# Five changes of order in a two-block transformer kernel: keys of the first group emptied earlier, a transpose between two halves of an up projection, two layer norms on POOL, one V projection in halves, the sigmoid moved up

## What is computed

```
block 0:  h = film(rmsnorm(x, norm1_w), cond, film1_w, film1_b)
          Q, K, V = h @ q_w + q_b, h @ k_w + k_b, h @ v_w + v_b       # one head of 128
          x = x + softmax(Q K^T * 128**-0.5) V @ proj_w + proj_b
          h = film(rmsnorm(x, norm2_w), cond, film2_w, film2_b)
          x = x + gelu(h @ mlp_w1 + mlp_b1) @ mlp_w2 + mlp_b2
block 1:  mod = silu(cond) @ ada_w.T + ada_b                          # six vectors per sequence
          h = layernorm(x) * (1 + scale_msa) + shift_msa
          x = x + gate_msa * (attention(h, 16 heads of 8, masked) @ proj_w.T + proj_b)
          h = layernorm(x) * (1 + scale_mlp) + shift_mlp
          x = x + gate_mlp * (gelu_tanh(h @ fc1_w.T + fc1_b) @ fc2_w.T + fc2_b)
```

## Time and profile before

| | us |
|---|---|
| median of 3 runs | 193.1 |
| lowest, highest | 192.03, 194.94 |
| the profiled execution | 191.69 |
| its span, first to last instruction | 189.9 |
| busy in the span: PE | 173.1 |
| PE weight loads | 134.2 |
| DVE | 121.1 |
| ACT | 107.7 |
| POOL | 98.7 |

### The profile page before, as it was taken

How to read it: one execution, slowest core, us unless ns; L and a number is a source line. 1 busy time by engine, 2 the same in 40 slices (tenths; PEclk the granted TensorE clock), 3 DMA queues, 4 the chain that set the end, 5 groups by cost and what they waited for, 6 DMA issues and landing times.

```text
span 189.9 us, 5687 instructions
## 1 busy us (share of the span) xinstructions
PE 173.1 (91%) x2250; PEld 134.2 (71%) x2250; DVE 121.1 (64%) x357; ACT 107.7 (57%) x272; POOL 98.7 (52%) x166
## 2 busy tenths in 40 slices
PE   6876989999699999889999999996997999999993
PEld 6744877587276698677678777875886765678592
DVE  0693598978005069768756876699489665596233
ACT  2336957862683751577577756673774785723500
POOL 5599949899900805994004333675145086691000
PEclk9999999999999999999999999998899999999999
DMA  5999999412650300300110000100000000001103
GB/s 126 345 430 423 433 412 431 177 43 52 217 224 0 114 0 3 116 5 5 57 60 3 7 35 31 57 5 2 5 7 7 2 3 0 5 0 55 59 0 110
DMA packets 5190, 19.31 MB, mean 102 GB/s; under 512 B 556, under 2 KB 1148, under 8 KB 3836
## 3 DMA queue, kind: packets, MB, share of 16 engines
q1 hardware_dynamic: 4844, 18.27, 25.0%
q10 hardware_dynamic: 320, 0.68, 1.2%
HBM read 7.24 MB, written 1.09 MB: 44 GB/s over the span
## 4 chain that ended last, share of the span: by engine, by line
PE 44%; issue 20%; POOL 19%; DVE 9%; DMA 3%; ACT 3%; POOLq 0%; DVEq 0%; ACTq 0%
PE ps L337 8%; PE ps L328 7%; PE ps L315 6%; PE ps L307 6%; POOL xb L1196 3%; POOL gtmp L1194 3%; POOL xc L1189 3%; PE ps L265 3%; POOL rstd L1115 3%; PE ps L366 2%; DMA xs<-x 2%; POOL xs L1203 2%; POOL gated L1200 2%; ACT hT L661 2%; DVE bn L844 2%
## 5 line engine op out<-in xcount | busy, mean ns | idle before, releaser
L1002 DVE TENSOR_REDUCE nm<-ps 128x4 f32<-128x512 f32 x64 | 42.0, 683 | 18.3 <-PE ps L366 17.9
L739 ACT ACTIVATE shared<-ps 128x512 f32<-128x512 f32 x64 | 34.5, 596 | 22.0 <-PE ps L366 21.9
L366 PE MATMUL ps<-k_pad,q_pad 32*128 32x128 f32 x512 | 35.4, 284 | 5.0 <-DVE nm L1002 4.7
L366 PEld LDWEIGHTS ps<-k_pad,q_pad 32*128 32x128 f32 x512 | 30.1, 188 | 13.2 <-issue 6.5
L366 PE MATMUL ps<-q_pad,k_pad 32*128 32x128 f32 x512 | 35.5, 285 | 0.1
L366 PEld LDWEIGHTS ps<-q_pad,k_pad 32*128 32x128 f32 x512 | 29.7, 188 | 0.5 <-DMA q_pad<-nmT 0.5
L1115 POOL TENSOR_TENSOR rstd<-var_eps,half 128x4 f32<-128x4 f32 x16 | 16.4, 1023 | 24.5 <-DVE var_eps L858 17.0
L1200 POOL TENSOR_TENSOR gated<-attn,gate 128x128 f32<-128x128 f32 x16 | 7.3, 459 | 40.8 <-ACT attn L758 40.7
L432 PE MATMUL ps<-shared,vx 128*32 128x128 f32 x512 | 17.9, 282 | 0.5 <-ACT attn L758 0.3
L785 ACT ACTIVATE hid<-ps,W 128x512 f32<-128x512 f32 x16 | 10.9, 689 | 9.7 <-PE ps L328 9.7
L307 PE MATMUL ps<-hT,W 128*128 128x512 f32 x32 | 14.6, 598 | 1.7 <-ACT hT L661 1.7
(11 more groups left out here) (127 smaller groups left out, 321.9 us busy)
## 6 DMA issues: line engine op xcount, KB each, us to landing
q_pad<-hid SPq DMA_DIRECT2D x1, 4096.0 KB, 21.7
k_pad<-hid SPq DMA_DIRECT2D x1, 4096.0 KB, 30.6
gate<-gates SPq DMA_DIRECT2D x1, 2048.0 KB, 7.2
xs<-x SPq DMA_DIRECT2D x4, 256.0 KB, 6.4
gate<-mask SPq DMA_DIRECT2D x1, 1024.0 KB, 11.9
q_pad<-apT SPq DMA_DIRECT2D x4, 256.0 KB, 2.4
k_pad<-apT SPq DMA_DIRECT2D x4, 256.0 KB, 2.4
W<-weights SPq DMA_DIRECT2D x1, 768.0 KB, 9.9
```

Of the source, the lines that this page charges most:

```text
L366: return mm(bank(to)[:, t], held[some, t, b], moved[some, t, b], start=True, stop=True, skip_group_check=True)
L739: a(pT[b % 2][:, r], bank(of), ACT.Exp, scale=HD ** -0.5).then_inc(s["c_exp"], 1)
L1002: v.tensor_reduce(nm[b % 2][:, 4 * r:4 * r + 4], bank(of), AX.X, ALU.max, negate=True).then_inc(s["c_max"], 1)
```

## The change

1. **Keys of group 0 sooner (ACT).** a_kv(0) goes ahead of the film of group 1.
2. **A turn between up chunks (PE and ACT).** Of the up projection of group 1 only chunks 0 and 1 come ahead of the transposes of group 2, chunks 2 and 3 behind them; on ACT the film of group 2 goes behind the second gelu of group 1.
3. **Two norms on POOL.** d_norm(0) and d_norm(1) leave DVE's steps 11 and 14; POOL does the same arithmetic (first_norm) at the end of its steps 11 and 15, and d_bias(0) moves to step 12.
4. **The second V in halves (PE and ACT).** V of group 1 is no longer one piece behind the second slot of step 2. Two matmuls of it stand in `between` of step 2 and two in that of step 3, ahead of turn_x, both into columns 0 to 255 of bank 7. ACT copies each half behind front_h of the same step. The second half has a wait for ACT's copy of the first; `behind` of step 3, which writes the same columns, now waits for the second copy.
5. **The sigmoid sooner (DVE).** Its three instructions go from behind the residual of group 0 to the place between the first norm and the first film of DVE.

The diff, without the list of semaphores:

```diff
 (PE)
-            def b_up(g):
-                for f in range(FC):
+            def b_up(g, fs=range(FC)):
+                for f in fs:
...
+            def second_value(half):
+                if half:
+                    pe.wait_ge(s["c_vh"], 1)
+                for j in (2 * half, 2 * half + 1):
+                    mm(ps[:, 7, N * (j % 2):N * (j % 2) + N], hc[1][:, j], w("v1"), start=True, stop=True,
+                       skip_group_check=True)
...
 between:
-                if g % G < 3 and g // G + 1 < B // G:
+                if g % G < 3 and g != 2 and g // G + 1 < B // G:
...
                 if b + LEAD < B:
                     pe.wait_ge(s["c_h"], b + LEAD)
+                    if b in (2, 3):
+                        second_value(b - 2)
                     turn_x(b + LEAD)
 behind:
-                    pe.wait_ge(s["c_v"], (b - 3) // G + 1)
+                    pe.wait_ge(s["c_v"], max(2, (b - 3) // G + 1))
 project:
-                if g < B // G and b % G < 3:
+                if g < B // G and b % G < 3 and b != 2:
...
-            b_up(1)
+            b_up(1, range(2))
             m_norm("b_", 2, 4)
+            b_up(1, range(2, FC))
             b_up(2)
 (ACT)
+            a_kv(0)
             affine("a_", 1, 0, bank(0))
-            a_kv(0)
             a_exp(0)
...
-            b_gelus(1)
+            b_gelus(1, range(2))
             affine("b_", 2, 1, bank(4))
+            b_gelus(1, range(2, FC))
             b_gelus(2)
...
+            def second_v(half):
+                v = ps[:, 7, 0:2 * N].rearrange("n (a k d) -> n a k d", k=2, d=HD)
+                slots = vx[1][:].rearrange("n b (a z) -> n (b a) z", z=64)[:, 16 * half:16 * half + 16]
+                for k in range(2):
+                    ins = a(slots[:, :, 48 * k:48 * k + HD], v[:, :, k], ACT.Copy)
+                ins.then_inc(s["c_v" if half else "c_vh"], 1)
...
 step:
                 if 0 < b and b + LEAD < B:
                     front_h(b + LEAD)
+                if b in (2, 3):
+                    second_v(b - 2)
...
-                elif b % G == 2 and b // G + 1 < B // G:
+                elif b % G == 2 and b > 2 and b // G + 1 < B // G:
                     front_v(b // G + 1)
 (DVE)
             ins.then_inc(s["a_xd"], 1)
+            dve.wait_ge(s["silu_e"], 1)
+            v.tensor_scalar(cond_s[:], cond_e[:], 1.0, None, ALU.add).then_inc(s["silu_one"], 1)
+            dve.wait_ge(s["silu_one"], 1)
+            v.reciprocal(cond_r[:], cond_s[:]).then_inc(s["silu_one"], 1)
+            dve.wait_ge(s["silu_one"], 2)
+            v.tensor_tensor(silu[:], w("cond", B), cond_r[:], ALU.mult).then_inc(s["silu_ok"], 1)
             dve.wait_ge(s["a_T"], 1)
... (the same six lines leave the place behind a_residual(0))
-                if b in (11, 14):
-                    d_norm((b - 11) // 3)
 (POOL)
+            def first_norm(g):
+                pool.wait_ge(s["d_pow"], g + 1)
+                for j in range(G):
+                    b = G * g + j
+                    ins = p.tensor_scalar(xn[g][:, j], xs[:, b], stat[:, b, 0:1], rstd[:, 3, b:b + 1], ALU.subtract, ALU.mult)
+                ins.then_inc(s["d_xn"], 1)
...
                 if b == 11:
+                    first_norm(0)
+                elif b == 12:
                     pool.wait_ge(s["c_xb"], b + 1)
                     d_bias(0)
+                elif b == 15:
+                    first_norm(1)
```

More of the change, by code:

```diff
@@ L150, in build @@
             b_pow b_xn b_xb b_T b_h b_M1 b_gelu b_M2 b_res
-            c_pow c_xb c_gp c_xc c_Tx c_h c_Q c_K c_V c_q c_k c_v c_qs c_ks
+            c_pow c_xb c_gp c_xc c_Tx c_h c_Q c_K c_V c_q c_k c_v c_qs c_ks c_vh
             c_S c_max c_NT c_nm c_nms0 c_nms1 c_T c_exp c_PV c_oT c_T2 c_rden c_on c_T3 c_onT c_pr c_at c_ga c_res c_st
@@ L695, in _, with b_gelus @@
                 a_exp(g)
-            def b_gelus(g):
-                for f in range(FC):
+            def b_gelus(g, fs=range(FC)):
+                for f in fs:
                     act.wait_ge(s["b_M1"], FC * g + f + 1)
@@ L725, in front_k @@
                 a(k_sb[:], bank(K_BANK[g]), ACT.Identity, bias=col("cols1", COL1["k_b"])).then_inc(s["c_k"], 1)
+            def second_v(half):
[4 more added lines that the diff above has]
+                ins.then_inc(s["c_v" if half else "c_vh"], 1)
             def front_v(g):
-                act.wait_ge(s["c_V"], g + 1)
+                act.wait_ge(s["c_V"], g + 1 if g < 2 else g)
                 v = ps[:, V_BANK[g], :].rearrange("n (a k d) -> n a k d", k=2, d=HD)
@@ L946, in _ @@
                 dve.wait_ge(s["a_res"], G * (g + 1))
[L947 to L954, removed]
             statistics(1, 3)
```

## The result

| | before | after |
|---|---|---|
| median, us | 193.1 (4 executions) | 183.64 (4 executions) |
| lowest, highest | 192.03, 194.94 | 182.89, 184.68 |
| profiled execution, its span | 191.69, 189.9 | 184.38, 182.6 |

The ratio of the times is 0.953 with a 95% interval of 0.945 to 0.962. The change makes the kernel 4.7% faster.

The account below looks back on a forecast made before the run. PE, busy 173.1 of 189.9 us, bounds the kernel, so only its waits count. Terms 2.0 + 1.65 + 0.2 + 3.2 + 1.1 = 8.15 us put the time between 183.5 and 184.95, at 184.3; range 181.9 to 188.2.

Parts of the forecast that it names:

- 1 and 5th move: First phase: keys first shortens the stall at the scores (1.45 us), earlier sigmoid removes a 0.6 us wait; 2.0 us together.
- The rival that the first phase gives its gain back: PE meets group 2's exponentials or DVE's statistics at their old finish; sum 6.15 us, time 185.5 to 187; chance 0.10.
- 2nd move: Up projection of group 1: PE's 1.74 us wait for group 2's film falls to 0.15; 1.65 us gained.
- 4. V in halves: Steps 2 and 3: splitting V of group 1 lets step 3's first slot start 0.2 us sooner.
- 5. Norms on POOL: Steps 12 and 15: PE's waits for maxima queued behind DVE's norms go, 1.95 + 1.25 = 3.2 us.
- The rival that POOL is late: Group 1's transposes: POOL's norm up to 3.2 us late, sum 5 us, time 186.7 to 188.1; chance 0.08.
- The rival that norms and maxima exclude each other: Steps 11 and 15: POOL's norms hold up DVE's maxima; kernel slower, 193.5 to 195 us; chance 0.07.
- 6. The clock: After step 12's 1.99 us stall: without it the clock does not fall, weighted values and transposes shorten; 1.1 us.
- The rival "the clock falls anyway": Clock falls regardless, or at another place; sum 7.05 us, time 184.6 to 186.1; chance 0.15.
- The sum: Whole kernel: 8.15 us gained; 183.5 from the profiled execution, 184.95 from the median, forecast set between at 184.3 us.

Follow-up runs that it names:

- experiment 5: Kernel before with only the keys of group 0 moved ahead, sigmoid in its old place; one execution, span 190.9 us, first queries to first up projection 22.34 us.
- experiment 10: Changed kernel with V of group 1 again in one piece, matmuls and copy; 183.77 us, ratio to before 0.958.
- experiment 7: Changed kernel with POOL doing the norm of group 1 twice, first into four unread tiles; one execution, 187.36 us.
- the norms alone: Kernel before with only the third move: both norms on POOL, bias of group 0 in step 12; 188.68 us, ratio 0.980 to before.
- the turn alone: Kernel before with only the second move: transposes of group 2 between up chunks of group 1; 189.51 us, ratio 0.986 to before.
- the bias later: Kernel before with only POOL's bias of group 0 moved from step 11 to 12, norms staying on DVE; 190.25 us, ratio 0.987 to before.
- the film shared: Changed kernel with DVE doing half of group 1's film in phase a; 183.23 us, then 183.16 in a second series beside the changed kernel's 183.01.
- experiment 8: Changed kernel with the last batch of dummy matmuls before the first transposes cut from 12 to 4; 184.19 us, ratio to before 0.962.
- all but the norms: Changed kernel with the third move undone: both norms back on DVE, POOL's bias in step 11; 187.12 us, ratio to before 0.975.
- after's second series: The changed kernel run once more, unaltered, beside later variants; 183.01 us (182.80 to 184.53).
- keys and sigmoid: Kernel before with only moves 1 and 5: keys of group 0 first, sigmoid sooner; 189.38 us, ratio 0.985 to before.

## Why the prediction was right

The time was put at 184.3 and came at 183.64, and in the profiled execution at 184.38. The steps, by their own numbers:

**1 and 5th move: 2.0 us.** 23.49 became 21.46, 2.03. The stall moved behind the scores and shrank to 0.80, by 1.54 to the queries (1.45 said). Its halves were wrong and made up for each other: not 1.45 and 0.6, but 1.15 and 0.88 (experiment 5). What was missed is that the memset doesn't move with DVE. The rival that the first phase gives its gain back did not come: the 2.03 are counted at the first up projection.

**2nd move: 1.65.** Counted from the first L265, the first slot of step 2 came at 63.09 instead of 66.84, 3.75 sooner, of which 2.03 is the gain of the moves above: 1.72. Alone it gave 1.6.

**4. V in halves: 0.2.** 0.18 where it was looked for; ACT's halves (0.45 each) and PE's lay in their waits, and the wait in `behind` never showed. But taken out of the whole the halves cost 0.7 to 0.8 (experiment 10), so for this change the term of 0.2, with nothing for what follows, was too small by some 0.5, by a cause that stays open.

**5. Norms on POOL: 3.2.** 3.2 by the slots (1.97 and 1.23), 3.3 to 3.4 alone or taken away. POOL's spare for group 1, put at 0.1, is 0.19. The rival that POOL is late did not come, and experiment 7 shows its mechanism and price: 2.9 us of stall for 3.1 of lateness, and a clock fall with it. The rival that norms and maxima exclude each other is refuted by the rows: 1.29 and 0.69 beside POOL's norm.

**6. The clock: 1.1.** From the second slot of step 12 to the film's wait behind it (L441, now L448) it is 4.36 us instead of 5.49, 1.13 less. Here the size was off for the median. The prediction worked from one profiled execution with one fall. By the list of executions before had, as read above, two falls in 17 of 31, and with the start that is not late they cost 2.2 to 2.6 us (191.1 to 191.5 against 188.9). The traces of the single moves show where the second can be: behind the first scores, at 16 to 20 us. The prediction argued that 2.27 us of idle PE was not followed by a lower clock; with the same code up to there it was, with the norms alone, the turn alone and the bias later. The rival "the clock falls anyway" did not come: in ten executions of after, and in 16 more with the film shared or V in one piece, whose longest stall is under 1 us from the first queries on too, the mean clock was never below 0.997. With less warming it was in three of four (experiment 8), so a fall needs no long stall behind the first queries if the start is another. That the stalls bring the falls is borne out for the kernels with the full warming, by how often falls come with and without them; in the four executions of all but the norms the 2.0 us stall brought none.

**The sum.** Without any fall the spans are 188.9 (a single execution) and 181.1: 7.8 us. The moves alone make 3.4 + 1.6 + 2.1, and the halves taken away 0.8: 7.9. The prediction's sum without its clock term is 7.05; the difference is mostly the 0.5 us of experiment 10, which the prediction did not have. With 2.3 us of clock, the cost of the falls in before's middle executions, the median falls by 10.1, and 193.1 less 10.1 is the 183.0 of after's second series. The first series, 183.64, has the lateness of the start in two of four executions. So the 184.3 was a little high: "executions with more stalls at the lower clock may be what lifts the median" was the right reason, with half its size; the value between 183.5 and 184.95 should have been the lower end.

## What to carry to other kernels

A DVE instruction of the kind of this norm or of the sigmoid's sum (a tensor_scalar from SBUF to SBUF) can take as long as POOL's instruction beside it; look in the rows of the engine for the same form at several durations. Here the norm has 1.08, 1.52 and 2.64, and 5.33 for group 3 in every kernel, where PE has no wait for it. Move one of the two where PE waits. A stall of some 2 us of an otherwise full PE cost more than its length in some executions here, so removing all such stalls is worth more in the median than one trace shows: read the mean clock of several executions. Tenths of a microsecond won at an early wait may be given back by the alignment of two engines later, so a small gain has to be read at the end of the span.

## What was not expected of the hardware

- A fall of the granted clock to its lower level, 1.2 of 2.4 GHz, came behind stalls of 2.0, 2.3 and 2.9 us in a part of the executions only: behind the one of 2.0 us of step 12 in profiled executions of before and of the kernels with keys alone or keys and sigmoid, and in none of the four of "all but the norms"; behind the 2.27 us at the first scores with the norms alone, the turn alone or the bias later, and not in the profiled execution of before. No trace has one behind the stalls of 1.3 and 1.7 us. With less warming falls came in three executions of four without such a stall in the one that has a trace; where they were is open.
- A POOL memset, which reads nothing, holds DVE off as its arithmetic does: 16 columns took 1.55 and 1.86 us beside it, 0.16 to 0.19 away from it.
- In after's profiled execution the matmuls up to 10.2 us took nearly twice the time that they take in its second, and everything started 1.5 us later. The dummy matmuls and the first transposes of after's first profiled execution, and of its second (after, again):

```profile
7.51 2.91 PE L245 MATMUL ps<-ident 128*128 128x128 f32 x12
...
10.21 0.72 PE L253 MATMUL ps<-ident,xn 128*128 128x128 f32 x4
```

```profile
6.61 1.58 PE L245 MATMUL ps<-ident 128*128 128x128 f32 x12
8.77 0.66 PE L253 MATMUL ps<-ident,xn 128*128 128x128 f32 x4 [0.57 <-POOL xn L1150]
```

The granted clock reads 1.00 in the windows of both. All traces begin with the slow matmuls (five of the first dummies in 1.27 us); five of the later ones take 0.72 in the second execution and in before. In the profiled executions of keys alone and of all but the norms the twelve dummies take 2.91 us as well, and the first queries come at 12.12 and 12.20 instead of 10.35 to 10.79. With less warming the first 20 dummies were as slow (4.64 us), yet the first queries came at 10.51; that is one execution. Spans some 1.5 us apart run through most of the kernels here; the cause was not tried beyond experiment 8 and stays open.
